# Sliding-window attention with a memory step: scores kept in one row of 128, transposes of probabilities moved ahead of the backward products, output projection as a split product

## The reference, cut to what matters

```python
q, k, v = (x_in @ w.T for w in (wq, wk, wv))          # 4 heads of 64
mask = (j <= i) & (j > i - 128)
logits = einsum('bhqd,bhkd->bhqk', q, k) / 8
attn = softmax(where(mask, logits, NEG))
out_swa = (attn @ v) @ wo.T
loss = 0.5 * sum((silu(x_in @ w1.T + b1) @ w2.T + b2 - out_swa) ** 2)
w1, b1, w2, b2 = (1 - alpha) * p - theta * grad(loss, p)
```

## Time and profile before

| what | value |
|---|---|
| time, median of 3 runs | 1868.12 us (1867.9 to 1870.27) |
| the profiled execution's own time | 1868.3 us |
| its span | 1866.6 us |
| mean granted TensorE clock | 0.993 |
| TensorE matmul busy | 1818.9 us, 97% |
| VectorE busy | 1231.6 us, 66% |
| ScalarE busy | 955.5 us, 51% |
| GpSimd busy | 950.5 us, 51% |

### The profile page before, as it was taken

One profiled execution on the slowest core, in us unless ns is written; L12 is line 12 of the kernel. 1 busy time (PEld: TensorE's weight loads), 2 busy tenths in 40 slices (PEclk: granted clock), 3 DMA queues, 4 the chain that ended last, 5 costly groups with the idle time before them and its releaser, 6 DMA issues.

```text
span 1866.6 us, 36384 instructions
## 1 busy us (share of the span) xinstructions
PE 1818.9 (97%) x12428; PEld 1604.3 (86%) x12428; DVE 1231.6 (66%) x2454; ACT 955.5 (51%) x1789; POOL 950.5 (51%) x667
## 2 busy tenths in 40 slices
PE   7999999999999999999999999999999999999995
PEld 5788888888888888777888878889999999999994
DVE  8877777777777777567776668844555555555552
ACT  6666666666666665554453454334344444444341
POOL 5666566666656666026666656655333333323234
PEclk9999999999999999999999999999999999999998
DMA  6211111111111110302111011268898988888883
GB/s 230 68 38 39 34 34 37 34 34 37 37 34 34 53 34 21 120 27 74 46 47 46 1 45 43 89 208 265 266 289 293 292 288 265 289 291 285 279 288 81
DMA packets 141016, 234.08 MB, mean 125 GB/s; under 512 B 24756, under 2 KB 88971, under 8 KB 140816
## 3 DMA queue, kind: packets, MB, share of 16 engines
q1 hardware_dynamic: 116368, 220.50, 34.4%
q0 software_dynamic: 24576, 12.69, 4.5%
HBM read 194.58 MB, written 78.45 MB: 146 GB/s over the span
## 4 chain that ended last, share of the span: by engine, by line
PE 44%; DMA 9%; issue 3%; POOL 1%; DVE 1%; POOLq 0%; ACT 0%; SPq 0%; DVEq 0%; ACTq 0%
PE bank L85 24%; PE bank L1905 15%; DMA out_rows<-c_y_rest,c_token_rest 9%; PE bank L1169 4%; POOL out_rows L2079 1%; PE bank L1668 1%; PE bank L2127 1%; DMA c_w<-in_e1T 0%; DMA slots<-last_row,last_index 0%; POOL slots L1864 0%; POOLq L2088 0%; POOLq L67 0%; PE bank L2138 0%; DVE early L1547 0%; POOLq L2213 0%
## 5 line engine op out<-in xcount | busy, mean ns | idle before, releaser
L1905 PE MATMUL bank<-c_xT,c_w 128*128 128x160 f32 x3072 | 429.6, 299 | 3.0 <-DMA c_w<-in_e1T 2.4
L1905 PEld LDWEIGHTS bank<-c_xT,c_w 128*128 128x128 f32 x3072 | 419.2, 190 | 4.1 <-DMA c_w<-in_e1T 3.1
L1864 POOL DMA_INDIRECT slots<-b_row,b_index x224 | 249.9, 1116 | 193.8 <-issue 117.1
L2079 POOL DMA_INDIRECT out_rows<-c_y,c_x x64 | 100.7, 1574 | 372.0 <-DMA out_rows<-c_y_rest,c_token_rest 249.4
L2027 DVE TENSOR_TENSOR c_gT<-bank,c_sil 128x480 f32<-128x480 f32 x128 | 84.2, 658 | 210.8 <-PE bank L1905 210.8
L1995 ACT CAST c_gTs_high<-c_gT 128x384 fp32r<-128x384 f32 x128 | 65.6, 513 | 135.6 <-DVE c_gT L2027 135.6
L1988 ACT ACTIVATE c_sil<-bank 128x480 f32<-128x480 f32 x128 | 73.1, 571 | 109.8 <-PE bank L1905 109.3
L2020 DVE TENSOR_TENSOR c_gTs_low<-c_gT,c_gTs_high 128x384 fp32r<-128x384 f32 x128 | 71.7, 560 | 75.4 <-ACT c_gTs_high L1995 75.4
L456 POOL TENSOR_TENSOR last_row<-last_row,a_e 128x256 f32<-128x256 f32 x33 | 54.4, 1648 | 124.1 <-DVE a_e L712 122.4
L85 PE MATMUL bank<-c_w2s_high,c_gTs_high 128*128 128x256 f32 x384 | 114.0, 297 | 0.9 <-DVE c_gTs_low L2020 0.9
L85 PE MATMUL bank<-c_w2s_high,c_gTs_low 128*128 128x256 f32 x384 | 107.0, 279 | 0.0
(11 more groups left out here) (329 smaller groups left out, 5451.3 us busy)
## 6 DMA issues: line engine op xcount, KB each, us to landing
c_w<-in_e1T SPq DMA_DIRECT2D x64, 1536.0 KB, 7.0
c_w<-in_e2T SPq DMA_DIRECT2D x48, 768.0 KB, 9.1
early<-in_e2T SPq DMA_DIRECT2D x16, 768.0 KB, 8.8
slots<-a_fill SPq DMA_DIRECT2D x16, 642.0 KB, 3.9
c_x<-slots SPq DMA_DIRECT2D x64, 160.5 KB, 8.4
a_x_in<-in_x SPq DMA_DIRECT2D x32, 128.0 KB, 2.1
xT_tiles<-a_xT SPq DMA_DIRECT2D x32, 128.0 KB, 1.7
swaT_tiles<-a_swaT SPq DMA_DIRECT2D x32, 128.0 KB
```

What stands on the lines that cost most here:

```text
L1864: pool.indirect_dma_start(out=T["slots"], out_offset=bass.IndirectOffsetOnAxis(ap=index[:, t, k:k + 1], axis=0), in_=row[:, t, :], in_offs ...
L1905: return nc.tensor.matmul(out, lhsT, rhs, start=first, stop=last, skip_group_check=True)
L2079: pool.indirect_dma_start(out=T["out"], out_offset=bass.IndirectOffsetOnAxis(ap=token, axis=0), in_=rows, in_offset=None, bounds_check=las ...
```

## The change

Only stage 1 is changed, in three parts.

First, the scores are kept in rows of 128 instead of 256. ScalarE copies the previous block's scores into `logit` (`previous_scores`), VectorE then overwrites them with the own block's where the key isn't later than the query (`copy_predicated` with the mask `own`). The scores are formed with the sign changed (`Q_SCALE` on the query), so that one minimum over the row gives the negated maximum, and the exponential is taken with scale -1. The multiplication by the reciprocal covers half the columns. After four transposes instead of eight, VectorE multiplies the result by 0/1 masks (`part_prob`), once for each block.

Second, from tile 2 on TensorE makes these transposes between `gradient` and `backward`, and VectorE makes `part_prob` between `modulate` and `grad_z`.

Third, the output projection is a split product: `woT` is split once, in tile 0, and attention's output `oT` in each tile, high part on ScalarE, low part on VectorE behind `turned_low`.

The diff has, after the tiles' declarations, GpSimd's part, ScalarE's, VectorE's and TensorE's, in this order.

```diff
-        masks = sb("masks", [P, 4, 2 * P])
+        own = sb("own", [P, 2, P], I32)
+        own_T = sb("own_T", [P, 2, P])
-        logit = sb("logit", [P, HEADS, 2 * P])
-        prob = sb("prob", [P, HEADS, 2 * P])
+        logit = sb("logit", [P, HEADS, P])
+        prob = sb("prob", [P, HEADS, P])
-        oT = sb("oT", [P, DC, P])
+        oT = split("oT", [P, DC, P])
...
+        def slot_scores(b, slot):
+            return psum[3 + b][:, :].rearrange("p (c t j) -> p c t j", c=DC, t=2)[:, :, slot, :]
...
-                pool.tensor_tensor(prob[:], prob[:], prec.unsqueeze(2).to_broadcast([P, HEADS, 2 * P]),
+                pool.tensor_tensor(prob[:], prob[:], prec.unsqueeze(2).to_broadcast([P, HEADS, P]),
                                    ALU.mult).then_inc(S("prob"), 1)
...
+                    pool.wait_ge(S("wo_high"), 1)
+                    pool.tensor_tensor(flat(woT[1][:]), flat(wo_raw[:]), flat(woT[0][:]).bitcast(F32), ALU.subtract)\
+                        .then_inc(S("wo_low"), 1)
...
+            def previous_scores(n, p):
+                act.wait_ge(S("s_mm"), n + 1)
+                first = P - MEM if not known(n, 2) else 0
+                for b in range(2):
+                    act.copy(logit[:, 2 * b:2 * b + 2, first:P], slot_scores(b, 1 - p)[:, :, first:P])\
+                       .then_inc(S("previous"), 1)
...
-                act.copy(flat(qT[0][:]), bank(0, D))
+                act.activation(flat(qT[0][:]), bank(0, D), ACT.Copy, scale=Q_SCALE)
...
                 act.copy(xms[q][0][:], xm[:]).then_inc(S("xm_high"), 1)
+                if known(n, 1):
+                    previous_scores(n, p)
...
-                    ins = act.activation(prob[:, s, :], logit[:, s, :], ACT.Exp, bias=npeak[:, s:s + 1],
+                    ins = act.activation(prob[:, s, :], logit[:, s, :], ACT.Exp, bias=npeak[:, s:s + 1], scale=-1.0,
...
-                act.wait_ge(S("probT_mm"), 2 * n + 2)
-                wait_past(act, S("o_mm"), n)
-                act.copy(flat(probT[:, 2:4, :, :]), bank(2)).then_inc(S("probT_hi"), 1)
...
                 if n is not LAST:
                     turned(n + 1)
+                act.wait_ge(S("o_mm"), n + 1)
+                wait_past(act, S("swa_mm"), n)
+                act.copy(flat(oT[0][:]), bank(5, D)).then_inc(S("oT_high"), 1)
...
+            def part_prob(n, p):
+                dve.wait_ge(S("probT_mm"), n + 1)
+                wait_past(dve, S("o_mm"), n)
+                for slot, part in ((p, 0), (1 - p, 1)):
+                    dve.tensor_tensor(probT[:, :, slot, :], bank(1).rearrange("p (s i) -> p s i", s=HEADS),
+                                      own_T[:, part, :].unsqueeze(1).to_broadcast([P, HEADS, P]), ALU.mult)\
+                       .then_inc(S("probT"), 1)
...
-                for s in range(HEADS):
-                    wait_past(dve, S("prob_exp"), n)
-                    wait_apart(dve, S("s_mm"), n + 1, S("passed_dve"))
-                    ins = dve.tensor_tensor_reduce(
-                        out=logit[:, s, :], in0=psum[3 + s // 2][:, (s % 2) * D:(s % 2 + 1) * D], in1=masks[:, mask, :],
-                        scale=float(DH) ** -0.5, scalar=-3e38, op0=ALU.add, op1=ALU.max, accum_out=peak[:, s:s + 1])
-                    if s % 2:
-                        ins.then_inc(S("peak"), 1)
-                dve.wait_ge(S("peak"), 2 * n + 2)
-                dve.tensor_scalar(npeak, peak, -1.0, None, ALU.mult).then_inc(S("npeak"), 1)
+                chosen = own[:, 0 if first else 1, :].unsqueeze(1).to_broadcast([P, DC, P])
+                wait_apart(dve, S("s_mm"), n + 1, S("passed_dve"))
+                for b in range(2):
+                    if not first:
+                        wait_apart(dve, S("previous"), 2 * n - 1 + b, S("passed_dve"))
+                    dve.copy_predicated(logit[:, 2 * b:2 * b + 2, :], chosen, slot_scores(b, p)).then_inc(S("picked"), 1)
+                dve.wait_ge(S("picked"), 2 * n + 2)
+                dve.tensor_reduce(npeak, logit[:], AX, ALU.min).then_inc(S("npeak"), 1)
...
                     modulate(n + 1)
+                if known(n, 2):
+                    part_prob(n, p)
                 if not first:
                     grad_z(n - 1)
-                dve.wait_ge(S("probT_mm"), 2 * n + 1)
-                wait_past(dve, S("o_mm"), n)
-                dve.tensor_copy(flat(probT[:, 0:2, :, :]), bank(1)).then_inc(S("probT_lo"), 1)
+                if not known(n, 2):
+                    part_prob(n, p)
...
-                dve.wait_ge(S("o_mm"), n + 1)
-                wait_past(dve, S("swa_mm"), n)
-                dve.tensor_copy(flat(oT[:]), bank(5, D)).then_inc(S("oT"), 1)
                 if n is not LAST:
                     turned_low(n + 1)
+                dve.wait_ge(S("oT_high"), n + 1)
+                wait_past(dve, S("swa_mm"), n)
+                dve.tensor_tensor(flat(oT[1][:]), bank(5, D), flat(oT[0][:]).bitcast(F32), ALU.subtract).then_inc(S("oT_low"), 1)
...
+            def turn_prob(n):
+                pe.wait_ge(S("prob"), n + 1)
+                if known(n, 2):
+                    pe.wait_ge(S("dW"), 4 * n - 7)
+                else:
+                    pe.wait_ge(S("v"), n + 1)
+                for head in range(HEADS):
+                    ins = turn(psum[1][:, head * P:(head + 1) * P], prob[:, head, :])
+                ins.then_inc(S("probT_mm"), 1)
...
                     gradient(n, q)
+                    turn_prob(n)
                 if not first:
                     backward(n - 1)
-                pe.wait_ge(S("prob"), n + 1)
-                for g in range(2):
...
-                    for b in range(4):
-                        ins = turn(psum[1 + g][:, b * P:(b + 1) * P],
-                                   prob[:, 2 * g + b // 2, (b % 2) * P:(b % 2 + 1) * P])
-                    ins.then_inc(S("probT_mm"), 1)
+                if not known(n, 2):
+                    turn_prob(n)
...
-                pe.wait_ge(S("oT"), n + 1)
+                pe.wait_ge(S("oT_low"), n + 1)
                 for k in range(DC):
-                    ins = mm(psum[7][:, D:2 * D], oT[:, k, :], woT[:, k, :], k == 0, k == DC - 1)
+                    ins = mm_split(nc, psum[7][:, D:2 * D], cut(oT, slice(None), k, slice(None)),
+                                   cut(woT, slice(None), k, slice(None)), k == 0, k == DC - 1)
```

More of the change, by code:

```diff
@@ L49 @@
 NEG = -1e30
+Q_SCALE = -float(DH) ** -0.5
 EPS = 1e-5
@@ L193, in memory_stage @@
         rstd = small[:, 0:TILES]
-        peak, npeak, psums, prec = (small[:, TILES + a * HEADS:TILES + (a + 1) * HEADS] for a in range(4))
+        npeak, psums, prec = (small[:, TILES + a * HEADS:TILES + (a + 1) * HEADS] for a in range(3))
         odd = 4 * UNIT + 2 * UNIT + 81 * UNIT + UNIT + 2 * P + UNIT
@@ L199, in memory_stage @@
         wqk = sb("wqk", [P, 2, DC, D])
-        woT = sb("woT", [P, DC, D])
+        wo_raw = sb("woT", [P, DC, D])
+        woT = split("woT", [P, DC, D])
         w2n = split("w2n", [P, DC, HID])
@@ L389, in _ @@
             for part in kT:
-                ins = pool.tensor_copy(part[:, :, 1, :], masks[:, 0, :].rearrange("p (c t) -> p c t", c=DC))
+                ins = pool.tensor_copy(part[:, :, 1, :], own_T[:])
             ins.then_inc(S("kv_zero"), 1)
+            pool.memset(own[:], 1)
             pool.wait_ge(S("kv_zero"), 1)
[L393 to L405, removed]
+            pool.memset(own_T[:], 1.0).then_inc(S("zeroed"), 1)
+            pool.wait_ge(S("zeroed"), 2)
+            pool.affine_select(out=own[:, 1, :], in_=own[:, 1, :], compare_op=ALU.is_ge, fill=0, base=0,
+                               pattern=[[-1, P]], channel_multiplier=1)
+            pool.affine_select(out=own[:, 0, :], in_=own[:, 0, :], compare_op=ALU.is_ge, fill=0, base=0,
+                               pattern=[[-1, P]], channel_multiplier=1)
+            pool.affine_select(out=own_T[:, 0, :], in_=own_T[:, 0, :], compare_op=ALU.is_ge, fill=0.0, base=0,
+                               pattern=[[1, P]], channel_multiplier=-1)
+            pool.affine_select(out=own_T[:, 1, :], in_=own_T[:, 1, :], compare_op=ALU.is_gt, fill=0.0, base=0,
+                               pattern=[[-1, P]], channel_multiplier=1).then_inc(S("banded"), 1)
+            pool.wait_ge(S("banded"), 1)
+            pool.memset(own[:, 0, 0:P - MEM], 0).then_inc(S("masks"), 1)
             pool.memset(e_sum[:], 0.0)
@@ L568, in body @@
                         weight_high(f"w2T_in{k}", w2T_raw[k], halves(w2T[0])[k])
-                act.wait_ge(S("probT_mm"), 2 * n + 2)
-                wait_past(act, S("o_mm"), n)
-                act.copy(flat(probT[:, 2:4, :, :]), bank(2)).then_inc(S("probT_hi"), 1)
+                    act.wait_ge(S("wo_in"), 16)
+                    act.copy(flat(woT[0][:]), flat(wo_raw[:])).then_inc(S("wo_high"), 1)
                 for g in range(2):
@@ L717, in body @@
                 first = not known(n, 1)
```

(9 more changed lines are left out.)

18 lines of the change are left out of this document (7 added, 11 removed).

## The result

The changed kernel takes 1853.13 us (median of 4 runs, 1851.57 to 1854.68) against 1868.77 us for the kernel before beside it: ratio 0.9914, 95% interval 0.9899 to 0.993. A second set of five runs gave 1850.64 us against 1869.96, ratio 0.9898 (0.988 to 0.9915). So it is faster by 0.9 to 1.0%, 16 to 19 us. The forecast was 1849.0 against a profiled 1868.3, which is 0.9897. The first set's median lies 4.1 us above the forecast, just outside the forecast's own range of 1846 to 1853 and inside the stated 1845.5 to 1859; the second set's lies inside both.

What follows compares the result with a forecast made beforehand. TensorE's queue was taken as the bound: 31 steady tiles x 0.61 us = 18.9, plus 0.4 in tiles 0 and 1, is 19.3 off 1868.3, so 1849.0 us; own range 1846 to 1853, wider range 1845.5 to 1859.

Steps and rivals of the forecast that it cites:

- Transposes: TensorE's transposes of probabilities, four instead of eight per tile at 0.109 us each: 0.435 us a tile goes.
- Projection: Output projection on TensorE: six split products, 0.68 us, replace two fp32 products, 0.86 us; 0.18 goes, bounds 0.14 to 0.20.
- The moved transposes: Four transposes placed between gradient and backward products on TensorE: the move costs nothing, 0.1 us as upper bound.
- The cover: Whether operands reach TensorE late: probabilities forecast 2.5 us early, h's low half 0.28 us early, so no stall.
- The two picks: VectorE's picks of 256 columns, each behind its ScalarE copy: taken at 0.42 us each, from above 0.84 each.
- a masked product: VectorE's 512-column product with a broadcast mask, two per tile: taken at 0.60 to 0.66 us, from above 0.84.
- The first low half of h's transpose: VectorE's output ahead of TensorE's prediction layer: forecast out at 314.95, 0.28 us before it is asked for.
- the narrow place: VectorE between gradient and prediction layer, with two masked products instead of one copy; margin 0.28 us.
- B: Rival, 15%: low half of h's transpose late on VectorE, 0.2 to 0.5 us a tile lost; 1860, from 1855 to 1865.
- C: Rival, 4%: each removed TensorE transpose gives back only its pass, 0.054 us; 0.39 a tile, 1856 in all.
- D: Rival, 4%: VectorE's picks and minimum cannot run beside GpSimd's addition; stall of 1.0 us a tile, 1880 in all.
- The start: Tiles 0 and 1, not bound by TensorE: 0.4 us gained, between 1.5 lost and 3 gained.

## Why the prediction was right

**What bounds it.** TensorE's queue set the tile before and sets it after: 21.14 us forecast, 21.16 measured, and each of the two terms put back alone costs about what it was said to bring.

**The terms.** Transposes: 0.435 forecast, 0.43 when doubled. Projection: 0.18 forecast within 0.14 to 0.20, 0.155 measured; its six products with the step into the next group take 0.70, not 0.68. The moved transposes: nothing was forecast for the step, and four of them with the first backward product take 0.68 (304.65 to 305.33) against 4 x 0.109 + 0.228 = 0.66. These hundredths, 0.02 to 0.03 a tile, make about 31 x 0.025 = 0.8 us.

**The cover.** The probabilities are ready 2.5 us ahead, as laid out. The two picks take 0.78 together, where 0.84 was forecast; a masked product starts 0.60 behind the one before, its lower bound. The first low half of h's transpose is out at 330.95 (330.26 + 0.69), and the prediction layer starts at 331.22: 0.27 us, where 0.28 was forecast. The two runs with more products measured the room from the other side: 0.60 more cost 0.23, so 0.37 of it were covered; the 0.27, and some of the 0.18 for which VectorE waited for ScalarE's high half. The layout also found the place that the move had to relieve: with the old order TensorE waits 0.45 us in each tile. The prediction named the narrow place but didn't say that, without the move, the rest of the change would have brought next to nothing.

**The rivals.** B did not occur, and its mechanism is real: it starts 0.4 us further on. C is excluded by the doubled transposes. D did not occur: picks and minimum ran beside the addition. The sign change put back shows what it would have cost in part: that instruction ends with GpSimd's addition, and a peak that comes 1.3 us later costs 0.13 a tile. By the Trainium skill ("SBUF — State Buffer", section "Who interferes with whom") tensor_reduce doesn't wait for GpSimd: the trace agrees (0.69 in the middle of the addition, 318.65 to 321.06). The page doesn't name the pick; here the two took 0.78 beside the addition. The same skill's "TensorE: Matmul & The Clock Gate", section "Terms", calls the transpose mode four times faster for fp32. By the rows an fp32 product of 128 columns takes about 0.215 (half of one of 256 columns) and one more transpose 0.107, with its weight load: half, not a quarter, and this is what a removed transpose gives back.

**The start.** The one step that was mis-sized: tiles 0 and 1 were forecast to gain 0.4 us, within 1.5 lost and 3 gained. The changed kernel's tile 3 began 1.6 us later than forecast in the first profile, so that tiles 0 and 1 lost 1.2 us, and 0.3 later in the second; against the kernel before's second profile (100.87), taken on the same chip, 98.99 is a gain of 0.7 in tiles 0 and 1. The forecast had no term for the granted clock: by the stretches above the two falls of the first profile cost 0.9 and 1.66, about 2.0 with what was made up behind them, which covers the 1.6. How near the total came, 1.6 us in one set and 4.1 in the other, is in part luck: where the clock falls moves a profile by 1 to 2 us, and nothing in the forecast says where. Stages 2 and 3 are unchanged: from the first product of stage 2 to the end it is 1866.6 - 754.06 = 1112.5 us before and 1849.8 - 737.28 = 1112.5 after; the second profiles have 1113.0 and 1112.7.

## What to carry to other kernels

Where one engine is busy without a gap, count its instructions by the distance between their starts, and the sum is the forecast; put each term back alone to see that they add. Then lay out one period for the engine with the least room behind it: what looks like 65% busy had 0.4 us of room in 21, and the order of two groups decided over 0.54 us, nearly as much as all the work removed (0.58). An instruction of four numbers can take over a microsecond if it waits for another engine's instruction; look at what ends when it ends. And compare the same stretch of work in two profiles before giving a loss in time, or a gain, to an edit: here falls of the clock hid one gain of 1.2 us and a slow start another.

## What the runs showed of the hardware

TensorE's granted clock fell to 0.50, its lower level of 1.2 GHz, in the first 60 us of both kernels, at places that differ from execution to execution: none in the kernel before's first profile, 22 to 26 and 50 to 53 us in its second; 38 to 42 and 52 to 56 in the changed kernel's first, 48 to 54 in its second. A fall of some 4 us costs 0.9 to 1.7 us of the work under it. In the changed kernel's second profile the fall began inside an idle stretch of 2.80 us (the wait for h until 48.35), in the first just behind one of 1.94 (until 37.81); but the kernel before idled 1.84 at the same place without a fall. What decides between them stays open.

At the very start the column of the clock can't be read. It shows 1.00 up to 12 us in every profile while products take about double: sixteen of `wqk` take 3.44 to 3.79 us at 5.7 to 6.0 us and 1.95 in later tiles. The kernel before's first profile shows 1.00 throughout, and yet its products of 512 columns start 0.43 us apart from 13.25 to 14.53, as in its second profile, which shows 0.50 there:

```profile
13.67 0.63 PE L85 MATMUL bank<-w1T_high,a_xT_low 128*128 128x512 f32 x1
14.10 0.63 PE L85 MATMUL bank<-w1T_high,a_xT_high 128*128 128x512 f32 x1
```

With the projection in fp32 again they do so until 17.7. So the stretch from 12 to 16 us is no difference between those executions; how long the half pace lasts is.

VectorE's instruction on four numbers took 0.17 us without GpSimd's addition beside it and up to 1.43 with it, while a minimum over 512 columns and the picks took 0.69 and 0.78 beside the same addition. A copy of 512 columns and a product of 512 columns with a broadcast mask cost VectorE the same 0.60 us from start to start.
